# A four-layer convolution and attention stack on one Trainium2 core: the first image tensor also passed in channels first, and the biases of the linear attention as one 512-column product a bank

## The chip, the cores and the metric

One core of a Trainium2 chip runs the whole program. The metric is the device time of one execution in microseconds (us). The kernel before takes 10623.62 us, the median of three runs (10621.04 to 10631.18).

## What is computed

Four images of 64 x 64 positions with 128 channels, in f32, pass through four layers; each adds its result to its input. The change touches the first two alone.

- Layer 0 is a deformable attention. The image is normalized by groups of channels, multiplied into queries, keys and values, filtered by a 3 x 3 filter per channel, and from the filtered queries come offsets and masks for 4 groups of 9 taps. Each position then gathers its 36 sampled points (4 corners each), scores them against its query, and sums the values.
- Layer 1 is a linear attention over the whole image, with a normalization of its own and one of its result.

```python
qkv = x @ w_qkv + b_qkv                      # layer 0, x normalized before
...
attn = softmax(einsum('bgnc,bgckn->bgnk', q * SCALE, sampled_keys))
out = einsum('bgnk,bgckn->bgnc', attn, sampled_values) @ w_proj + b_proj
...
qkv = einsum('bhwc,cf->bhwf', x, w_qkv)      # layer 1, x normalized before
q = softmax(q, -1) * 32 ** -0.5; k = softmax(k, 1); v = v / n
context = einsum('bnhd,bnhe->bhde', k, v)
out = einsum('bhde,bnhd->bnhe', context, q) @ w_out + b_out
```

Layer 1 has no bias of its own on q, k and v; the one in the kernel comes from the normalization, whose mean is taken off behind the product instead of ahead of it.

## The kernel before, in words

`first_layers` (line 118) does layers 0 and 1. Its main loop runs over 128 tiles of 128 positions, 32 tiles an image. In each tile:

- POOL (line 467, `tile`) issues 36 indirect DMAs, which gather the sampled records into `rec[t % 2]`. With two such buffers, the gather of tile t may start once DVE has summed tile t-2, that is, at the end of line 935.
- DVE works on the gathered tile: keys by query (line 920), their sum (921), the scores (up to 925); then it waits for ACT's exp (line 706, `prob`), and goes on with line 928 to the sum of the values (line 935, `att_t`).
- PE turns and projects the result (lines 603 to 606), DVE adds the input (line 942), ACT stores it (line 712).

After each tile every engine takes one step of a side program, by `next(side)`. `sides` (line 313) gives its order: in the 32 tiles of image b there are first the 19 gaps of `points(b + 1)` (all that layer 0 needs before the gathers of the next image), and then the 11 gaps of `linear(b - 1)` (layer 1 of the image before). So `points(1)`, `points(2)` and `points(3)` have their gap 0 behind tiles 0, 32 and 64, and their gap 1 behind tiles 1, 33 and 65. `points(0)` runs ahead of the tiles as a prologue, and `linear(3)` behind them as an epilogue. `linear(0)` starts behind tile 51; its gap 7, with the "o" banks, lies behind tile 58.

Side work on PE and ACT is a list of jobs, each with its gap (`opening` and `beside` for layer 0, `lj` for layer 1). A job is one PSUM bank of 512 columns: PE fills bank `ps[n % 4]`, ACT copies it out, and PE may write that bank again once ACT has copied job n-4. In its own program ACT takes all copies of a gap before the exp of the next tile.

Jobs that the text speaks of:

- "x" (layer 0, gap 0): 4 PE transposes a bank (line 503) from the tokens `a_tok`, 8 banks, copied by ACT (line 631) to the image by channels `a_chan`. Out of it DVE takes the statistics in gap 1 (`spread`, line 726; bn_stats is line 729).
- "qkv" (layer 0, gap 1): 24 banks of one product each (line 514), copied by ACT (line 636). They wait for `spread`.
- "qv" (layer 1, gaps 1 to 4; 3, 5, 5 and 3 banks): two products of 256 columns (line 567), each followed by a product that adds the bias `brow` by a row of ones (line 568), copied by ACT (line 684).
- "o" (layer 1, gap 7; 8 banks): four products of 128 columns (line 594), each followed by one that adds the bias `bl_s` (line 595), copied by ACT (line 689).

Of the kernel before, what the change touches and what calls it, by code (L numbers as in the profile page):

```python
# [12 lines left out]
ACT = mybir.ActivationFunctionType  # L13
AX = mybir.AxisListType.X

P = 128
BATCH, H, W, C = 4, 64, 64, 128
N = H * W
# [99 lines left out]
def first_layers(nc, A, x, records, meta, mid, out):  # L118
# [9 lines left out]
    with ExitStack() as ctx:  # L128
# [10 lines left out]
        a_tok = tiles_at(R1)  # L139
# [55 lines left out]
        brow = st.sb("brow", [1, 2, C])  # L195
# [91 lines left out]
        opening = [("x", g, 0) for g in range(NG)]  # L287
        opening += [("qkv", (f, g), 1) for f in range(3) for g in range(NG)]
# [46 lines left out]
        def _(sp):  # L335
# [7 lines left out]
            def points(b):  # L343
# [4 lines left out]
                for r in (slice(0, P // 2), slice(P // 2, P)):  # L348
                    sp.dma_start(a_tok[r, :, :], batch(x, b)[r, :, :]).then_inc(a_x, 16)
# [132 lines left out]
        def _(pe):  # L482
# [3 lines left out]
            def points(b):  # L486
                done_act, done_offs, pj = b * PA, b * NG, plan(b)
                for gap in range(PG):
                    for n, (kind, at, own) in enumerate(pj):
# [10 lines left out]
                        if kind == "x":  # L500
                            pe.wait_ge(a_x, b * 80 + 80)
                            for t in range(4):
                                last = pe.transpose(bank[:, t * P:t * P + P], a_tok[:, 4 * at + t, :], id_s[:, :])
                        if kind == "qkv":
                            f, g = at
                            if n == NG:
# [33 lines left out]
            def linear(b):  # L540
                pe.wait_ge(l_x, b * 96 + 96)
                pe.wait_ge(l_act, b * LJ)
                for gap in range(LG):
                    for n, (kind, g, own) in enumerate(lj):
# [18 lines left out]
                        if kind == "qv":  # L563
                            for t in range(2):
                                o = bank[:, t * 256:t * 256 + 256].rearrange("p (f d) -> p f d", f=2)
                                i = 2 * g + t
                                pe.matmul(o, l_chan[:, i * P:i * P + P], lw_s[:, 0:3:2, :], start=True, stop=False)
                                last = pe.matmul(o, ones[:, :], brow[:, :, :], start=False, stop=True)
# [16 lines left out]
                        if kind == "o":  # L585
                            if g == 0:
                                pe.wait_ge(l_blk, b + 1)
                                pe.matmul(ps_c[:, P:2 * P], blocks[:, :], wo_s, start=True, stop=True).then_inc(l_mix, 1)
                                pe.wait_ge(l_mixc, b + 1)
                                pe.wait_ge(l_act, b * LJ + FIRST["o"])  # L590
                            for t in range(4):
                                i = 4 * g + t
                                o = bank[:, t * P:t * P + P]
                                pe.matmul(o, l_chan[:, i * P:i * P + P], mix, start=True, stop=False)
                                last = pe.matmul(o, ones[:, :], bl_s, start=False, stop=True)
# [15 lines left out]
        def _(act):  # L611

            def points(b):
                pj = plan(b)
                for gap in range(PG):
# [9 lines left out]
                    for n, (kind, at, own) in enumerate(pj):  # L625
# [4 lines left out]
                        if kind == "x":  # L630
                            ins = act.activation(a_chan[:, at * 512:at * 512 + 512], bank[:, :], ACT.Copy)
                        if kind == "qkv":
                            f, g = at
                            if n == NG:
                                act.wait_ge(a_norm, 2 * b + 2)
# [83 lines left out]
        def _(dve):  # L719
# [5 lines left out]
            def spread(sums, values, chain, act_sem, act_base, stat, gsum, var, std, nm, norm, pair, mean, cell, source):  # L725

                for g in range(NG):
                    dve.wait_ge(act_sem, act_base + g + 1)
# [37 lines left out]
            def points(b):  # L766
# [3 lines left out]
                spread(stats, a_chan, step_a, a_act, b * PA, a_stat, a_gsum, a_var, a_std, a_nm, a_norm, m2, mv, sc, b)  # L770
# [83 lines left out]
            def linear(b):  # L854
                yield
                spread(stats, l_chan, step_l, l_act, b * LJ, l_stat, l_gsum, l_var, l_std, l_nm, l_norm, m2, mv, sc, b)
# [3 lines left out]
                dve.tensor_copy(brow[:, :, :], ps_s[0:1, 128:512].rearrange("p (f d) -> p f d", f=3)[:, 0:3:2, :]).then_inc(l_norm, 1)  # L860
# [31 lines left out]
                dve.sem_inc(l_blk, 1)  # L892
                dve.wait_ge(l_mix, b + 1)
# [1450 lines left out]
def l0_arrays(i):  # L2344
    a = {n: np.asarray(i["L0_conv_" + n]) for n in ("w_qkv", "b_qkv", "w_dw", "b_dw", "pconv_off_w", "w_off", "b_off", "pconv_mask_w", "w_mask", "b_mask", "w_proj", "b_proj")}
    return dict(
# [93 lines left out]
```

## Time and profile before

| | |
|---|---|
| runs | 10623.62 us median of 3 (10621.04 to 10631.18) |
| the profiled execution | 10620.11 us, its span 10618.3 us |
| prologue (`points(0)`) | 0 to 317 us |
| the 128 tiles with their side work | 317 to 7618 us |
| epilogue (`linear(3)`) | 7618 to 7860 us |
| layers 2 and 3 | 7860 to 10618 us |
| busy over the span | PE 3786.1, DVE 5654.4, ACT 1430.5, POOL 4571.0 us |

The span runs from the first to the last instruction on the chip; the execution's own time is 1.8 us longer. Times in rows are counted from the start of the span. The timeline gives for an instruction its start, its duration, engine, line and operation, then how long the engine had been idle before it and what ended that. A releaser named "remote" or "issue" is one that the profile does not tie to an instruction of another engine.

### The profile page before, as it was taken

To read this page: it belongs to the slowest core of one execution; us is meant where nothing else is said; L and a number is where in the kernel's file an instruction comes from. 1 tells how busy PE (TensorE), PEld (TensorE's weight loads), DVE (VectorE), ACT (ScalarE), POOL (GpSimd) and SP (SyncE) were. 2 spreads that over 40 slices of the span, in tenths; PEclk is the share of its full clock that TensorE was granted. 3 is DMA by queue.
4 is the path that set the end of the run, shared out by engine and by line. 5 is a ranking of instruction groups with operands and counts; after the bars stand their busy time and mean duration, and the time that the engine had idled before them with its cause. 6 is when DMAs were issued, how large, how long until landed. Compare 5 with 4: busy or idle time off the path is not lost. (4 is left out here: it accounts for less than half of the span.)

```text
span 10618.3 us, 108724 instructions
## 1 busy us (share of the span) xinstructions
PE 3786.1 (36%) x42948; PEld 2618.7 (25%) x42948; DVE 5654.4 (53%) x6585; ACT 1430.5 (13%) x2619; POOL 4571.0 (43%) x4748
## 2 busy tenths in 40 slices
PE   5113100012202211130132132000267568699997
PEld 3001100000201110020111011000134346588885
DVE  5275754556664554657455445544444356455554
ACT  1000000000000000000000000000012133344442
POOL 0565667755565555656564564777400000000000
PEclk6555555555555555555555555555566778899998
DMA  4433363323336233424632332333220533222224
GB/s 78 115 100 84 96 161 104 108 81 101 83 107 149 82 88 92 110 74 108 151 92 78 97 90 79 106 100 100 66 41 0 195 68 78 78 67 67 65 67 168
DMA packets 973814, 1001.49 MB, mean 94 GB/s; under 512 B 417257, under 2 KB 794962, under 8 KB 969298
## 3 DMA queue, kind: packets, MB, share of 16 engines
q0 software_dynamic: 221184, 604.27, 19.6%
q1 hardware_dynamic: 703106, 350.65, 13.9%
q10 hardware_dynamic: 49104, 40.35, 1.3%
q8 instruction: 339, 5.55, 0.2%
q14 instruction: 81, 0.66, 0.0%
HBM read 797.88 MB, written 190.61 MB: 93 GB/s over the span
## 5 line engine op out<-in xcount | busy, mean ns | idle before, releaser
L467 POOL DMA_INDIRECT l_rec<-records,l_row x4608 | 4514.9, 980 | 3071.4 <-issue 1530.4
L603 PE MATMUL l_pso<-l_id,l_att_t 128*128 128x128 f32 x128 | 60.3, 471 | 5129.3 <-DVE l_att_t L935 2818.4
L603 PEld LDWEIGHTS l_pso<-l_id,l_att_t 128*128 128x128 f32 x128 | 23.7, 185 | 5176.5 <-DVE l_att_t L935 2850.6
L920 DVE TENSOR_TENSOR l_rec<-l_rec,l_psv 128x4608 f32<-128x4608 f32 x128 | 634.0, 4953 | 1024.3 <-DMA l_rec<-records,l_row 944.8
L935 DVE TENSOR_REDUCE l_att_t<-l_rec 128x128 f32<-128x4608 f32 x128 | 1004.4, 7847 | 4.4
L2191 DVE COPY l3p_mix<-l3p_ps 128x512 f32<-128x512 f32 x1024 | 660.0, 686 | 577.8 <-PE l3p_ps L2067 577.8
L928 DVE TENSOR_REDUCE l_total<-l_prob 128x4 f32<-128x36 f32 x128 | 24.4, 191 | 1626.9 <-ACT l_prob L706 1483.9
L2153 ACT ACTIVATE l3p_mix<-l3p_ps 128x512 f32<-128x512 f32 x1024 | 556.6, 596 | 664.1 <-PE l3p_ps L2067 664.1
L933 DVE TENSOR_TENSOR l_rec<-l_rec,l_psv 128x4608 f32<-128x4608 f32 x128 | 634.0, 4953 | 4.4
L921 DVE TENSOR_REDUCE l_dots<-l_rec 128x144 f32<-128x4608 f32 x128 | 634.0, 4953 | 4.4
L2067 PE MATMUL l3p_ps<-l3p_psi,l3p_ms 32*128 32x128 f32 x16384 | 611.7, 283 | 22.2 <-DVE l3p_mix L2191 17.4
L2067 PEld LDWEIGHTS l3p_ps<-l3p_psi,l3p_ms 32*128 32x128 f32 x16384 | 518.7, 186 | 181.7 <-ACT l3p_mix L2153 109.0
L2028 POOL COPY l3p_four<-l3p_fil 128x128 f32 (+1 forms) x64 | 18.7, 292 | 1199.5 <-PE l3p_psm L2120 1198.0
L764 DVE SCALAR_TENSOR_TENSOR l_psc<-l_area,l_wd,l_psc 128x512 f32<-128x512 f32 x504 | 381.0, 756 | 17.9
L706 ACT ACTIVATE l_prob<-l_score 128x36 f32<-128x36 f32 x128 | 29.5, 230 | 2544.7 <-DVE l_score L925 774.2
L2017 POOL MEMSET l3p_xs<- 128x4096 f32 x1 | 3.5, 3511 | 849.2 <-POOLq L55 849.2
L1386 POOL MEMSET l2b_res<- 128x512 f32 x1 | 0.5, 524 | 720.3 <-POOLq L55 720.3
L708 ACT ACTIVATE l_att_c<-l_pso 128x128 f32<-128x128 f32 x128 | 35.5, 277 | 2039.3 <-PE l_pso L603 1164.7
L942 DVE TENSOR_TENSOR l_done<-l_pso,l_res 128x128 f32<-128x128 f32 x128 | 37.4, 292 | 500.8 <-PE l_pso L606 393.0
L2084 PE MATMUL l3p_psy<-l3p_mix,l_mats 128*32 128x128 f32 x8192 | 259.7, 273 | 1.1 <-ACT l3p_yr L2162 0.8
L2084 PE MATMUL l3p_psy<-l3p_mix,l3p_xs 128*32 128x128 f32 x8192 | 259.0, 273 | 0.2 <-issue 0.2
L2084 PEld LDWEIGHTS l3p_psy<-l3p_mix,l_mats 128*32 128x32 f32 x8192 | 217.3, 108 | 21.1 <-issue 1.3
(360 smaller groups left out, 7230.7 us busy)
## 6 DMA issues: line engine op xcount, KB each, us to landing
l_rec<-records,l_row POOLq DMA_INDIRECT x4608
records<-l_area SPq DMA_DIRECT2D x96, 512.0 KB
l2b_w<-l_w SPq DMA_DIRECT2D x32, 1024.0 KB, 10.8
l_row<-meta SPq DMA_DIRECT2D x128, 154.0 KB
l_area<-x SPq DMA_DIRECT2D x16, 1024.0 KB
records<-l_rec SPq DMA_DIRECT2D x32, 512.0 KB
l_x_hat<-l3a_xout ACTq DMA_DIRECT2D x32, 512.0 KB, 4.2
l3p_xin<-l_x_hat SPq DMA_DIRECT2D x128, 128.0 KB, 3.1
```

The source lines that it names most:

```text
L467: pool.indirect_dma_start(out=rec[s % 2][:, k, :], out_offset=None, in_=records[b].rearrange("o g y x c d -> (o g y x) (c d)"), in_offset= ...
L603: pe.transpose(ps_a, att_t[:, :], id_s[:, :]).then_inc(s_att, 1)
L764: step_a(dve.scalar_tensor_tensor(acc if t < TAPS - 1 else to, window(f, g, t), wd_s[:, f, t:t + 1], acc, ALU.mult, ALU.add))
L920: step(dve.tensor_tensor(keys, keys, asked.broadcast_to([P, GROUPS, TAPS * CORNERS, HC]), ALU.mult))
L921: step(dve.tensor_reduce(flat, rec[two][:, :, :].rearrange("p k (c d) -> p (k c) d", c=CORNERS)[:, :, 0:HC], AX, ALU.add))
L933: step(dve.tensor_tensor(values, values, ps_w.rearrange("p (g m) -> p g m", g=GROUPS).unsqueeze(3).broadcast_to([P, GROUPS, TAPS * CORNERS ...
L935: step(dve.tensor_reduce(att_t[:, :].rearrange("p (g d) -> p g d", g=GROUPS), values.rearrange("p g m d -> p g d m"), AX, ALU.add))
L942: step(dve.tensor_tensor(done[two][:, :], ps_p, res[two][:, :], ALU.add))
L2067: mm = pe.matmul(bank.rearrange("p (x c e) -> p x c e", x=2, e=2)[:, i // 2, :, i % 2], ms[32 * g:32 * g + 32, 4 * q + i, :], psi[s][32 * ...
L2084: mm = pe.matmul(ps_y[32 * g:32 * g + 32, c, :], flat[:, 32 * m - 8 * r:32 * m - 8 * r + 32], mix[s][:, :, 2 * m + kind, :], start=r == 0 ...
L2153: act.activation(mix[t.side(0)][:, x:x + 2, :, :].rearrange("p x c e -> p (x c e)"), ps[(2 * q + h) % 3][:, 0, :], ACT.Copy).then_inc(s_se ...
L2191: dve.tensor_copy(mix[t.side(0)][:, x:x + 2, :, :].rearrange("p x c e -> p (x c e)"), ps[(2 * q + h) % 3][:, 1, :]).then_inc(s_setd, 1)
```

## The change

First part: a new input `x_chan` is the same image tensor, with channels first, laid out on the host. SP loads it straight to `a_chan` (two transfers of 64 rows with 16 KB a row, in place of two from `x` in pieces of 512 bytes). The 8 "x" jobs of each image, 32 transposes and 8 copies, are gone. DVE's `spread` waits for the load instead of ACT's copies, and the first "qkv" job carries the waits that job 8 had.

Second part: in the linear attention a bank gets its bias by one product of 512 columns ahead of the others. For "qv" that is 1 + 2 products in place of 4, for "o" 1 + 4 in place of 8. The bias row is therefore held twice (`brow`, two copies) and four times (`orow`, a new copy on DVE in gap 7, before its wait for `l_mix`); both rows now lie in parts of `area` that are free then. The columns that PE writes in a bank, 1024 with the bias, stay as they were.

```diff
@@ -192,7 +191,8 @@
         wo_s, ls_s, bl_s = wq_s[:, 0:C], wq_s[:, C:2 * C], wq_s[0:1, 2 * C:3 * C]
-        brow = st.sb("brow", [1, 2, C])
+        brow = area[0:1, 5 * N:5 * N + 4 * C].rearrange("p (t f d) -> p t f d", t=2, f=2)
+        orow = area[0:1, 2 * N:2 * N + 4 * C].rearrange("p (t d) -> p t d", t=4)
         bcol = st.sb("bcol", [P, 1])
@@ -284,8 +284,7 @@
         PG, LG = 19, 11
-        opening = [("x", g, 0) for g in range(NG)]
-        opening += [("qkv", (f, g), 1) for f in range(3) for g in range(NG)]
+        opening = [("qkv", (f, g), 1) for f in range(3) for g in range(NG)]
         opening += [("qt", g, 6) for g in range(NG)]
@@ -346,7 +345,7 @@
                 for r in (slice(0, P // 2), slice(P // 2, P)):
-                    sp.dma_start(a_tok[r, :, :], batch(x, b)[r, :, :]).then_inc(a_x, 16)
+                    sp.dma_start(a_chan[r, :], x_chan[b, r, :]).then_inc(a_x, 16)
                 sp.dma_start(wq_s[:, :], A["l0_w_qkv"]).then_inc(a_x, 16)
@@ -497,13 +496,10 @@
                             pe.wait_ge(a_act, done_act)
-                        if kind == "x":
-                            pe.wait_ge(a_x, b * 80 + 80)
-                            for t in range(4):
-                                last = pe.transpose(bank[:, t * P:t * P + P], a_tok[:, 4 * at + t, :], id_s[:, :])
                         if kind == "qkv":
                             f, g = at
-                            if n == NG:
+                            if n == 0:
+                                pe.wait_ge(a_x, b * 80 + 80)
                                 pe.wait_ge(a_stat, b + 1)
@@ -561,11 +557,11 @@
                         if kind == "qv":
+                            pe.matmul(bank[:, :], ones[:, :], brow[:, :, :, :].rearrange("p t f d -> p (t f d)"), start=True, stop=False)
                             for t in range(2):
...
                                 i = 2 * g + t
-                                pe.matmul(o, l_chan[:, i * P:i * P + P], lw_s[:, 0:3:2, :], start=True, stop=False)
-                                last = pe.matmul(o, ones[:, :], brow[:, :, :], start=False, stop=True)
+                                last = pe.matmul(o, l_chan[:, i * P:i * P + P], lw_s[:, 0:3:2, :], start=False, stop=t == 1)
                         if kind == "kt":
@@ -586,13 +582,12 @@
                                 pe.matmul(ps_c[:, P:2 * P], blocks[:, :], wo_s, start=True, stop=True).then_inc(l_mix, 1)
-                                pe.wait_ge(l_mixc, b + 1)
+                                pe.wait_ge(l_mixc, 2 * b + 2)
                                 pe.wait_ge(l_act, b * LJ + FIRST["o"])
+                            pe.matmul(bank[:, :], ones[:, :], orow.rearrange("p t d -> p (t d)"), start=True, stop=False)
                             for t in range(4):
                                 i = 4 * g + t
-                                o = bank[:, t * P:t * P + P]
-                                pe.matmul(o, l_chan[:, i * P:i * P + P], mix, start=True, stop=False)
-                                last = pe.matmul(o, ones[:, :], bl_s, start=False, stop=True)
+                                last = pe.matmul(bank[:, t * P:t * P + P], l_chan[:, i * P:i * P + P], mix, start=False, stop=t == 3)
                         last.then_inc(l_job, 1)
@@ -627,11 +622,9 @@
                         bank = ps[n % NB]
-                        if kind == "x":
-                            ins = act.activation(a_chan[:, at * 512:at * 512 + 512], bank[:, :], ACT.Copy)
                         if kind == "qkv":
                             f, g = at
-                            if n == NG:
+                            if n == 0:
                                 act.wait_ge(a_norm, 2 * b + 2)
@@ -722,10 +715,10 @@
 
-            def spread(sums, values, chain, act_sem, act_base, stat, gsum, var, std, nm, norm, pair, mean, cell, source):
+            def spread(sums, values, chain, ready, start, per, stat, gsum, var, std, nm, norm, pair, mean, cell, source):
 
                 for g in range(NG):
-                    dve.wait_ge(act_sem, act_base + g + 1)
+                    dve.wait_ge(ready, start + per * g)
                     ins = dve.bn_stats(sums[:, g, :], values[:, g * 512:g * 512 + 512])
@@ -767,7 +760,7 @@
                 yield
-                spread(stats, a_chan, step_a, a_act, b * PA, a_stat, a_gsum, a_var, a_std, a_nm, a_norm, m2, mv, sc, b)
+                spread(stats, a_chan, step_a, a_x, b * 80 + 80, 0, a_stat, a_gsum, a_var, a_std, a_nm, a_norm, m2, mv, sc, b)
                 dve.tensor_scalar(wn_s[:, :], wq_s[:, :], sc[:, 2:3], None, ALU.mult).then_inc(a_norm, 1)
@@ -853,11 +846,13 @@
                 yield
-                spread(stats, l_chan, step_l, l_act, b * LJ, l_stat, l_gsum, l_var, l_std, l_nm, l_norm, m2, mv, sc, b)
+                spread(stats, l_chan, step_l, l_act, b * LJ + 1, 1, l_stat, l_gsum, l_var, l_std, l_nm, l_norm, m2, mv, sc, b)
                 dve.tensor_scalar(lw_s[:, :, :], w_s[:, :, :], sc[:, 2:3], None, ALU.mult).then_inc(l_norm, 1)
...
                 dve.tensor_copy(bcol[:, :], ps_s[:, 2:3]).then_inc(l_norm, 1)
-                dve.tensor_copy(brow[:, :, :], ps_s[0:1, 128:512].rearrange("p (f d) -> p f d", f=3)[:, 0:3:2, :]).then_inc(l_norm, 1)
+                for t in range(2):
+                    ins = dve.tensor_copy(brow[:, t, :, :], ps_s[0:1, 128:512].rearrange("p (f d) -> p f d", f=3)[:, 0:3:2, :])
+                ins.then_inc(l_norm, 1)
                 yield
@@ -890,6 +885,7 @@
                 dve.sem_inc(l_blk, 1)
+                dve.tensor_copy(orow, bl_s.unsqueeze(1).broadcast_to([1, 4, C])).then_inc(l_mixc, 1)
                 dve.wait_ge(l_mix, b + 1)
@@ -2343,8 +2339,9 @@
     a = {n: np.asarray(i["L0_conv_" + n]) for n in ("w_qkv", "b_qkv", "w_dw", "b_dw", "pconv_off_w", "w_off", "b_off", "pconv_mask_w", "w_mask", "b_mask", "w_proj", "b_proj")}
+    x_chan = np.asarray(i["x"]).reshape(BATCH, N, C).transpose(0, 2, 1)
     return dict(
-        l0_w_qkv=a["w_qkv"], l0_b_qkv=a["b_qkv"].reshape(3, P).T, l0_w_dw=a["w_dw"].reshape(3 * C, TAPS), l0_b_dw=a["b_dw"].reshape(3, P).T,
+        x_chan=x_chan, l0_w_qkv=a["w_qkv"], l0_b_qkv=a["b_qkv"].reshape(3, P).T, l0_w_dw=a["w_dw"].reshape(3 * C, TAPS), l0_b_dw=a["b_dw"].reshape(3, P).T,
         l0_pconv_off=a["pconv_off_w"].transpose(4, 2, 3, 0, 1).reshape(3 * HC, 3, GROUPS * HC),
```

How the change moves instructions on ACT, from the end of tile 0 to the "qkv" copies of image 1 (before it `l_prob` is the exp of a tile, `l_att_c` and `l_psv` are copies of the tile loop, the DMA is the tile's store). Before:

```order
L706 ACTIVATE l_prob<-l_score 128x36
L708 ACTIVATE l_att_c<-l_pso 128x128
L699 ACTIVATE l_psv<-l_row 128x128
L712 DMA x<-l_done 128x128
L631 ACTIVATE l_area<-l_ps 128x512 x8
L706 ACTIVATE l_prob<-l_score 128x36
L708 ACTIVATE l_att_c<-l_pso 128x128
L699 ACTIVATE l_psv<-l_row 128x128
L712 DMA x<-l_done 128x128
L618 ACT_TABLE_LOAD
L618 ACTIVATE l_sc<-l_sc 128x1
L636 ACTIVATE l_area<-l_ps,l_bn 128x8x64 x24
```

With the change:

```order
L699 ACTIVATE l_prob<-l_score 128x36
L701 ACTIVATE l_att_c<-l_pso 128x128
L692 ACTIVATE l_psv<-l_row 128x128
L705 DMA x<-l_done 128x128
L699 ACTIVATE l_prob<-l_score 128x36
L701 ACTIVATE l_att_c<-l_pso 128x128
L692 ACTIVATE l_psv<-l_row 128x128
L705 DMA x<-l_done 128x128
L613 ACT_TABLE_LOAD
L613 ACTIVATE l_sc<-l_sc 128x1
L629 ACTIVATE l_area<-l_ps,l_bn 128x8x64 x24
```

The eight copies between the store of tile 0 and the exp of tile 1 are gone; the 24 "qkv" copies stand where they stood, between tile 1 and tile 2.

On PE, the start of the "o" job (gap 7 of `linear`; the first row is the projection of the tile before, the second the product for `mix`). Before, with the last two rows repeated:

```order
L606 MATMUL l_pso<-l_bo,l_ones 128x128
L588 MATMUL l_psc<-l_wq,l_blocks 128x128
L594 MATMUL l_ps<-l_area 128x128
L595 MATMUL l_ps<-l_wq,l_ones 128x128
L594 MATMUL l_ps<-l_area 128x128
L595 MATMUL l_ps<-l_wq,l_ones 128x128
```

With the change, again with the last two repeated:

```order
L601 MATMUL l_pso<-l_bo,l_ones 128x128
L584 MATMUL l_psc<-l_wq,l_blocks 128x128
L587 MATMUL l_ps<-l_area,l_ones 128x512
L590 MATMUL l_ps<-l_area 128x128 x4
L587 MATMUL l_ps<-l_area,l_ones 128x512
```

Eight products a bank have become five, in the same place.

## Rows read from the trace of the kernel before

**Rows 1.** Stretches of the span: start:end, us, then busy us (instructions) of PE, PEld, DVE, ACT, POOL, granted clock, DMA share, GB/s.

```profile
317.00:7618.00 7301.00, 1253.29 (x3376) 734.52 (x3376) 4004.85 (x2957) 374.25 (x814) 4514.86 (x4608) 0.52 0.37 100
7618.00:7860.00 242.00, 147.54 (x440) 88.00 (x440) 61.56 (x151) 44.67 (x64) 0.00 (x0) 0.58 0.16 31
```

**Rows 2.** Timeline of DVE in a tile without side work.

```profile
6934.21 4.95 DVE L920 TENSOR_TENSOR l_rec<-l_rec,l_psv 128x4608 f32<-128x4608 f32 x1 [22.28 <-DMA l_rec<-records,l_row]
6945.65 0.19 DVE L928 TENSOR_REDUCE l_total<-l_prob 128x4 f32<-128x36 f32 x1 [0.37 <-ACT l_prob L706]
...
6985.05 4.95 DVE L920 TENSOR_TENSOR l_rec<-l_rec,l_psv 128x4608 f32<-128x4608 f32 x1 [22.75 <-DMA l_rec<-records,l_row]
```

**Rows 3.** The page's costliest groups: busy us, mean ns | idle before, releaser.

```profile
L928 DVE TENSOR_REDUCE l_total<-l_prob 128x4 f32<-128x36 f32 x128 | 24.4, 191 | 1626.9 <-ACT l_prob L706 1483.9
```

**Rows 4.** Timeline of ACT between the tiles 0 and 1.

```profile
392.84 0.60 ACT L631 ACTIVATE l_area<-l_ps 128x512 f32<-128x512 f32 x1 [2.48 <-issue]
...
463.80 0.60 ACT L631 ACTIVATE l_area<-l_ps 128x512 f32<-128x512 f32 x1 [6.41 <-remote]
464.29 0.22 ACT L706 ACTIVATE l_prob<-l_score 128x36 f32<-128x36 f32 x1
```

**Rows 5.** Timeline of DVE: start of tile 1.

```profile
409.24 4.95 DVE L920 TENSOR_TENSOR l_rec<-l_rec,l_psv 128x4608 f32<-128x4608 f32 x1 [17.10 <-DMA l_rec<-records,l_row]
```

**Rows 6.** Timeline of POOL: first issues of tiles 3, 4, 35 and 67.

```profile
478.74 0.94 POOL L467 DMA_INDIRECT l_rec<-records,l_row  x1 [26.48 <-DVE l_att_t L935]
...
558.51 0.94 POOL L467 DMA_INDIRECT l_rec<-records,l_row  x1 [35.08 <-DVE l_att_t L935]
...
2224.45 0.95 POOL L467 DMA_INDIRECT l_rec<-records,l_row  x1 [21.18 <-DVE l_att_t L935]
...
4133.64 0.94 POOL L467 DMA_INDIRECT l_rec<-records,l_row  x1 [34.45 <-DVE l_att_t L935]
```

**Rows 7.** Timeline of POOL: an issue within tile 34.

```profile
2200.78 1.10 POOL L467 DMA_INDIRECT l_rec<-records,l_row  x1 [0.30 <-issue]
```

**Rows 8.** Timeline of ACT, gap 1: "qkv" copies of images 1 and 2.

```profile
493.51 0.69 ACT L636 ACTIVATE l_area<-l_ps,l_bn 128x512 f32<-128x512 f32 x1 [4.61 <-PE l_ps L514]
495.22 0.69 ACT L636 ACTIVATE l_area<-l_ps,l_bn 128x512 f32<-128x512 f32 x1 [1.02 <-issue]
...
509.01 0.69 ACT L636 ACTIVATE l_area<-l_ps,l_bn 128x512 f32<-128x512 f32 x1 [4.91 <-remote]
...
543.37 0.23 ACT L706 ACTIVATE l_prob<-l_score 128x36 f32<-128x36 f32 x1
...
2259.37 1.27 ACT L636 ACTIVATE l_area<-l_ps,l_bn 128x512 f32<-128x512 f32 x2 [25.30 <-remote]
```

**Rows 9.** Timeline of ACT and POOL: "o" copies of image 0, and tile 61.

```profile
3733.78 0.60 ACT L689 ACTIVATE l_area<-l_ps 128x512 f32<-128x512 f32 x1 [13.49 <-remote]
3760.39 1.08 ACT L689 ACTIVATE l_area<-l_ps 128x512 f32<-128x512 f32 x2 [26.02 <-remote]
...
3779.27 0.60 ACT L689 ACTIVATE l_area<-l_ps 128x512 f32<-128x512 f32 x1 [5.19 <-PE l_ps L595]
...
3794.81 0.94 POOL L467 DMA_INDIRECT l_rec<-records,l_row  x1 [40.50 <-DVE l_att_t L935]
```

**Rows 10.** Timeline of ACT: a "qv" copy of gap 2 and one of the epilogue.

```profile
3452.45 0.60 ACT L684 ACTIVATE l_area<-l_ps 128x512 f32<-128x512 f32 x1 [18.32 <-remote]
...
7726.11 0.60 ACT L684 ACTIVATE l_area<-l_ps 128x512 f32<-128x512 f32 x1 [4.00 <-PE l_ps L568]
```

**Rows 11.** Timeline of PE in layer 2: bias of 512 columns, then products of 128.

```profile
7907.52 2.07 PE L1085 MATMUL l2a_ps<-l2a_brow,l2a_ones 1*128 1x512 f32 x2
7909.52 2.08 PE L1088 MATMUL l2a_ps<-l2a_wkv,l2a_chan 128*128 128x128 f32 x8
```

**Rows 12.** Timeline of PE and DVE in the prologue.

```profile
21.54 5.91 PE L503 MATMUL l_ps<-l_id,l_area 128*128 128x128 f32 x32 [21.54 <-DMA l_bo<-l_b_proj]
...
23.43 1.44 DVE L729 BATCH_NORM_STATS2 l_stats<-l_area 128x6 f32<-128x512 f32 x2 [23.43 <-ACT l_area L631]
```

More of the change, by code:

```diff
@@ L115, in token_norm, with first_layers @@
     step(ins)
-def first_layers(nc, A, x, records, meta, mid, out):
+def first_layers(nc, A, x, x_chan, records, meta, mid, out):
     AHEAD = 4
@@ L136, in tiles_at @@
             return area[:, start:start + N].rearrange("p (t c) -> p t c", c=C)
-        a_tok = tiles_at(R1)
         a_chan = area[:, R2:R2 + N]
@@ L2356, in layers01 @@
     meta = nc.dram_tensor("meta", (BATCH, NT, P, META), F32).ap()
-    first_layers(nc, A, x, records, meta, mid, out)
+    first_layers(nc, A, x, A["x_chan"], records, meta, mid, out)
 def l1_arrays(i):
```

## The prediction, made before the changed kernel ran

> **What bounds the kernel now.** I read the stretches first, since the change touches only layers 0 and 1. The 128 tiles take 7301 us, in which POOL is busy for 4515 and DVE for 4005; the epilogue takes 242 [rows 1]. A tile without side work shows the beat: DVE starts on the next one 50.84 us later and has then waited 22.75 us for gathered data [rows 2]. The gathers set the pace there; DVE's 28 us fit inside. The beat itself is POOL's issue: 36 issues at 0.95 + 0.30 us make 45.0 us [rows 6], and at 1.10 + 0.30 they make 50.4 us [rows 7].
>
> But 128 tiles at 45 to 50 us are 5760 to 6450 us, not 7301. The rest is in the groups by cost: DVE's line 928 waits 1483.9 us for ACT's exp [rows 3], where a tile without side work has 0.37 us of it [rows 2]. ACT is not busy then (374 us in 7301 [rows 1]). The timeline of ACT shows what it does: between the tiles it stands at its side copies, and the exp is queued behind them. In gap 0 the eight "x" copies last from 392.84 to 464.40, and the exp of tile 1 follows at once [rows 4], though DVE had started on that tile at 409.24 [rows 5]. POOL may gather tile 3 only once tile 1 is summed, so it pauses for 26.48 us [rows 6]. That chain (side copies, exp, sum, gather) is what the change can shorten: not the busy time, but the pauses of POOL.
>
> The copies are slow in a way that the busy time does not explain. During POOL's issues of a tile a bank of one "qkv" product comes every 5.60 us (4.91 idle + 0.69), but every 1.71 us at the start of the gap, where POOL has only just begun [rows 8]. Of banks with more instructions, an "o" bank of eight products comes after 13.49 to 26.02 us idle while POOL issues, and after 5.19 once it has stopped [rows 9]. So I read it as a price for each PE instruction while gathers are issued, which is lifted soon after POOL stops: POOL stopped at 3794.81 - 40.50 = 3754.31, and two "o" copies came at 3760.39, 6 us later [rows 9].
>
> **The change, part by part.**
>
> *Prologue.* PE starts its "x" transposes at 21.54, released by the constants, and DVE its statistics at 23.43 behind the first copy [rows 12]. Without them DVE starts at 21.54, and the copies' beat no longer stretches it: 1.9 us and about 1, so -3 (0 to -6, as all of PE's x work is 5.91 [rows 12]). It is first in a serial chain, so it counts in full.
>
> *Gap 0 of images 1 to 3.* 8 copies and 32 transposes go. What lies behind them is the exp of the next tile. A free tile takes 11.44 us from line 920 to line 928 [rows 2]; from the exp to the next gather it takes 478.74 - 464.29 = 14.45 [rows 4, 6]. Tile 1 is thus summed at 409.24 + 11.4 + 14.5 = 435.1 instead of 478.7. POOL ends tile 2 at 478.74 - 26.48 = 452.26 [rows 6] and goes straight on: 26.2 us less. Late next is gap 1: the exp of tile 2 stands behind 24 "qkv" copies. It came at 543.37 [rows 8], 19.9 us after POOL's last issue of tile 3 (558.51 - 35.08 = 523.43 [rows 6]). Those copies now start 44 us earlier, while the end of tile 3's gather is 26 us earlier, so at least as many are through when POOL stops, and the next pause stays 35 us. Two things may take back a little. The first copy came 14.8 us after the pause ended in image 1 (493.51 - 478.74) and 34.9 us after it in image 2 (2259.37 - 2224.45) [rows 6, 8]; with the longer lead, three banks more are left when POOL stops, about 3 us. And a tile may be gathered at the longer beat, 5.4 us. I take 26 - 3 = 23 for image 1; for image 2 the pause is 21.2, and the copies have 25 us more of room, 22; for image 3 the pause is 34.5 [rows 6], less 3 and 5.4, 26. Together -71. Bounds: all of the pauses and 9 us in image 2 (28.8 us from POOL's stop to the exp there against 19.9), -91; for the other end see the first rival.
>
> SP's loads stay two transfers of 1 MB in sum, at the same place of its program and in longer pieces; they were hidden behind tiles and stay so. The load lies a tile ahead of gap 0, and `spread` a tile behind it: two tiles for a load that now must be there one tile earlier. I cost it at nothing.
>
> *"o" banks, linear(0) to linear(2).* After POOL stopped, copies came at 3760.39 (two) and the last at 3779.27, the last 5.19 + 0.60 = 5.79 us behind the one before it; 3761.5 to 3779.3 holds three such steps [rows 9]; the exp, the sum and POOL followed, with a pause of 40.50. With five instructions a bank in place of eight, a bank takes 5/8 of the time under the gather. From 3733.78 to 3754 that lets at least one or two more through, and of four banks that PE may run ahead all are done at the stop. I take the last three as gone: 3 x 5.79 = -17 each. If only their own length shrinks (below), it is 3 x 1.79 = -5.
>
> *"qv" banks.* Three instructions for four. The fifth bank of gap 2 came after 18.32 us of idle time [rows 10]; a quarter of that is 4.6, in each of two gaps of five banks. Part goes into pauses that others set, so -3 an image (+3 to -13; `brow` costs DVE a copy more, and it is on the chain of gap 1; nearest rows: 0.19 us for a small operation, 0.7 for 512 columns [rows 3, 12]). The new `orow` copy lies while DVE waits for PE's `mix` anyway.
>
> Three images at -17 - 3: -60 (bounds -6 and -90).
>
> *Epilogue, linear(3).* Here nothing gathers, PE is the bound (147.5 of 242 us [rows 1]) and ACT waits for each bank: a "qv" bank comes every 4.00 + 0.60 = 4.60 us [rows 10], an "o" bank every 5.79 [rows 9]. Both write 1024 columns, bias included. What the new form takes is in layer 2, where a bias of 512 columns takes 2.00 us to the next instruction, and four products of 128 columns (two records each) 2.08 [rows 11], so 4.0 us a bank. The clock is 1.2 GHz in both. That is 16 x 0.6 = 9.6 and 8 x 1.79 = 14.3, less some at the higher clock and 0.4 for the copy: -22 (-15 to -25).
>
> A rule speaks against this part. The Trainium skill ("TensorE: Matmul & The Clock Gate", Back-to-back issue gap) gives the gap between products as columns by the clock, N / 1.2 ns cold, whatever their number. By that rule 1024 columns cost the same in two pieces or eight, and part two is worth nothing. The rows disagree: 5.79, 4.60 and 4.0 us for the same columns [rows 9, 10, 11].
>
> **Sum:** -3 - 71 - 60 - 22 = -156. The profiled execution takes 10620.1, so 10464; the median lies 3.5 above that execution, hence **10467 us**.
>
> **Rivals.**
> 1. *The wait comes back in the next gap.* Where POOL no longer pauses before tile 3, none of the "qkv" copies falls into the free time behind a pause, in which they came every 1.71 us. Five of them must then run after the stop, 5 x 1.71 = 9 us an image: -17 - 12 - 25 = -54. In "o" the banks only shrink, -16 in sum. With -3 and -22: -95, 10529. For it: 25.30 us of idle before the copies of image 2 [rows 8]. Against it: 44 us of head start for 26.
> 2. *Columns alone are the price.* Part two gives nothing, -74 remain: 10550. Against it the three bank times above.
> 3. *All clean*, every bound at its good end: -6 - 91 - 90 - 22 = -209, 10414.
> 4. *Slower: the longer beat.* The gather has two beats, 45.0 and 50.4 us a tile. By the mean busy time of an issue, 4514.86 / 4608 = 0.980 [rows 1], between 0.945 and 1.10, some 22% of the tiles have the longer one. If pauses are what keeps the beat short, fewer pauses make more long tiles. At 156 / 5.4 = 29 tiles more the gain is gone; with 48 more it is 259 - 156 = +103, 10727. For it: the quiet tiles at 6934 us have the long beat [rows 2]. Against it: even in the tiles at 6934 us POOL needs no pause to issue 36 times, and the mean of 0.980 us says that three tiles in four have the short beat now, most of them with no pause just ahead, since DVE holds POOL up in a few gaps an image only.
> 5. *No effect:* the pauses are filled by whatever comes next (the "qkv" gap swallows all of gap 0's gain, and the gap of the token norm that of "o"); only the epilogue and prologue count, -25: 10599, just outside 0.2%; with a little lost elsewhere, "same".
>
> **How the numbers follow.** The forecast has 0.45, rival 1 0.24, rival 2 0.12, rival 3 0.09, rival 5 0.05, rival 4 0.05. The range takes in the first four and their bounds: 10400 to 10560. Within 0.2% (21 us, about what a measurement can tell from no change) lies part of rival 5 and some mixture with rival 4: 0.04. Slower by more: 0.04. Faster: 0.92.
>
> **What the changed profile would show.** Right: no wait of line 928 in tiles 1, 33 and 65, and no POOL pause before tiles 3, 35 and 67; the pauses before tiles 4, 36 and 68 about as long as before; the last "o" copy of linear(0) 6 us or less after POOL's stop, and tile 61's pause some 23 us; in the epilogue 4.0 us a bank of "qv" and of "o", and a stretch of about 220 us. The wait of line 928 for exp would fall from 1484 us by some 44 x 3 + 17 x 3 and more. Wrong: pauses before tiles 4, 36, 68 longer by what the earlier ones lost (rival 1 or 5), epilogue banks still at 5.79 (rival 2), a mean POOL issue above 0.98 us (rival 4).

## The result and the profile after

The changed kernel takes 10537.33 us, the median of four runs (10513.33 to 10541.06), against 10622.33 us (four runs); the ratio is 0.9914, 95% interval 0.9901 to 0.9926. That is 85 us less; 156 us less were forecast. The time lies in the range, 8 us above that of rival 1.

The two traces can be set side by side stage by stage (the end of a stage is that of its last DVE instruction):

| stage | before | after | difference | forecast |
|---|---|---|---|---|
| prologue, to the keys of tile 0 | 364.0 | 359.7 | -4.3 | -3 |
| `points(1)` to `points(3)`, from the end of tile 0, 32, 64 to that of tile 2, 34, 66 | | | -14.7, -7.9, -12.0 | -71 |
| "qv" gaps of linear(0) to linear(2), tiles 54 to 57, 86 to 89, 99 to 102 | | | +8.9, +12.5, +6.4 | -9 |
| "o" gaps, tiles 59, 91, 104 (the pauses are before tiles 61, 93, 106) | | | -17.5, -15.6, -17.0 | -51 |
| all 128 tiles to the end of tile 127 | 7254.0 | 7204.5 | -49.5 | -131 |
| epilogue, to the end of layer 1 | 210.0 | 178.9 | -31.1 | -22 |
| layers 2 and 3, not touched | 2790.3 | 2796.1 | +5.8 | 0 |

The parts of the tiles add up to -57; +7 us come in steps of under 2 us in other tiles. The stretch of the tiles in the changed kernel, in the columns of [rows 1], and DVE's wait for exp (us in total, times, longest):

```profile
317.00:7564.20 7247.20, 1175.89 (x3040) 659.68 (x3040) 4007.81 (x2963) 358.26 (x788) 4526.39 (x4605) 0.52 0.37 101
```

```profile
DVE l_total L924 <- ACT l_prob L699: 1489.1, 65, 66.7
```

The wait of DVE for exp did not fall: 1489 us where it was 1483.9 [rows 3]. The prediction said that it would fall by over 180. What was taken from some tiles came back in others.

POOL's first issues of tiles 4, 36, 57, 61 and 68, in this order by time, answer to [rows 6, 9]:

```profile
539.45 0.94 POOL L466 DMA_INDIRECT l_rec<-records,l_row  x1 [46.30 <-DVE l_att_t L931]
...
2287.68 0.94 POOL L466 DMA_INDIRECT l_rec<-records,l_row  x1 [50.42 <-issue]
...
3504.89 0.94 POOL L466 DMA_INDIRECT l_rec<-records,l_row  x1 [26.95 <-DVE l_att_t L931]
...
3761.62 0.94 POOL L466 DMA_INDIRECT l_rec<-records,l_row  x1 [23.05 <-DVE l_att_t L931]
...
4166.40 0.94 POOL L466 DMA_INDIRECT l_rec<-records,l_row  x1 [50.07 <-DVE l_att_t L931]
```

There is no row for tiles 3, 35 and 67, since their pauses are gone (26.5, 21.2 and 34.5 us [rows 6]), as forecast. But the next pause of each image grew: before tile 4 from 35.1 to 46.3, before tiles 36 and 68 from 44.1 and 33.8 to about 50. Two pauses together went from 61.6 to 46.6 in image 1. In images 2 and 3, tiles 35 and 67 also got the longer beat (49.4 and 49.9 us for 44.7), which took 5 to 7 us back in each. Tile 57 has a pause of 26.95 where it had 7.6, and tile 61 one of 23.05 for 40.50 [rows 9]: the one is the loss at "qv", the other the gain at "o".

ACT's timeline in gap 1 of image 1 shows where the next pause grew ([rows 8] before):

```profile
464.12 1.84 ACT L629 ACTIVATE l_area<-l_ps,l_bn 128x512 f32<-128x512 f32 x3 [23.62 <-remote]
...
471.76 0.69 ACT L629 ACTIVATE l_area<-l_ps,l_bn 128x512 f32<-128x512 f32 x1 [4.91 <-PE l_ps L510]
...
508.86 0.69 ACT L629 ACTIVATE l_area<-l_ps,l_bn 128x512 f32<-128x512 f32 x1 [4.91 <-remote]
...
524.30 0.23 ACT L699 ACTIVATE l_prob<-l_score 128x36 f32<-128x36 f32 x1
```

Tile 1 was summed at 430.1, 5 us earlier than forecast (4 of them because tile 1 itself starts earlier, with the prologue), but the first copy came 34 us later (464.12), not 14.8. DVE's statistics themselves were as quick as before: from the first bn_stats to line 97 they took 8.4 us in both kernels. What came late is behind them: twelve memsets (8.9 us in place of 1.2) and the last small DVE instruction ahead of the copies, which waits for a short product of PE. In image 2 this way was as long before (35 us). The last instruction, before, then with the change:

```profile
492.87 0.16 DVE L779 TENSOR_TENSOR l_bn<-l_pss,l_bq 128x3 f32<-128x3 f32 x1 [1.33 <-DVE l_area L776]
```

```profile
461.96 0.16 DVE L772 TENSOR_TENSOR l_bn<-l_pss,l_bq 128x3 f32<-128x3 f32 x1 [9.62 <-remote]
```

That still leaves no fewer copies done when POOL stops: 8, 11 and 10 of the 24 in images 1 to 3, where it was 8, 4 and 8. The loss comes after the stop. POOL's last issue of tile 3 ends at 493.2; the copies go on at 5 us a bank until 508.86, and the exp comes 31 us behind the stop, where it was 19.9. In images 1 to 3, copies still came 4 us or more apart up to 16, 21 and 22 us after the stop, in the kernel before up to 2, 10 and 2 us. What differs ahead of the stop is for how long POOL had issued without a pause: four tiles, 16 and 6 with the change, one tile in each image before. In the middle of this late stretch no gather is issued and no byte is moved (columns of [rows 1]):

```profile
498.00:508.00 10.00, 4.15 (x4) 1.00 (x4) 0.00 (x0) 1.38 (x2) 0.00 (x0) 0.50 0.00 0
```

PE is busy for 4.15 of these 10 us, so its own work does not fill them either. Whatever holds up the short instructions outlasts the gathers themselves; what it is, no run shows.

The "qv" gaps show another way to lose a pause ([rows 10] before). Gap 2, then gap 3, of linear(0):

```profile
3409.57 0.60 ACT L677 ACTIVATE l_area<-l_ps 128x512 f32<-128x512 f32 x1 [3.41 <-issue]
...
3455.71 0.60 ACT L677 ACTIVATE l_area<-l_ps 128x512 f32<-128x512 f32 x1 [16.20 <-remote]
```

The banks of gap 2 now all come at 4.0 us, so tile 54 ends 18 us earlier, and POOL goes on to tile 56 without a pause (10.5 before). Then the second and third bank of gap 3 come 16.8 us apart and the fourth after 13.3; before, its first four came at 4.6. Tile 55 loses 27.

In the epilogue, a "qv" copy early and late, and the last "o" copy ([rows 9, 10] before):

```profile
7606.66 0.60 ACT L677 ACTIVATE l_area<-l_ps 128x512 f32<-128x512 f32 x1 [1.51 <-PE l_ps L564]
...
7656.16 0.60 ACT L677 ACTIVATE l_area<-l_ps 128x512 f32<-128x512 f32 x1 [3.41 <-PE l_ps L564]
...
7714.53 0.60 ACT L682 ACTIVATE l_area<-l_ps 128x512 f32<-128x512 f32 x1 [3.41 <-PE l_ps L590]
```

Both bank kinds take 4.01 us, as the price from layer 2 said [rows 11]; the first five "qv" banks ran at the higher of TensorE's two clocks, 2.1 us each, where the kernel before had two such (2.3 and 2.5 us).

### The profile page after: what moved, and what is told of

Its sections match the earlier page's. It is cut to its first block and busy times, and to the rows that moved or that the text cites. A ratio compares the mean times of both kernels' runs of the same rounds, so it can differ in the third digit from the quotient of the medians.

```text
span 10539.2 us, 107779 instructions
## 1 busy us (share of the span) xinstructions
PE 3679.2 (35%) x42500; PEld 2522.4 (24%) x42500; DVE 5657.8 (54%) x6593; ACT 1410.3 (13%) x2586; POOL 4585.7 (44%) x4748
```

## Experiments

Runs were taken in sets, each with the kernel before beside the new kernels. The next four kernels ran on the chip with number 11; the number for the first result is not known.

**Part one alone.** The changed kernel with the bias products, `brow` and `orow` as before:

```diff
-                            pe.matmul(bank[:, :], ones[:, :], brow..., start=True, stop=False)
+                                last = pe.matmul(o, ones[:, :], brow[:, :, :], start=False, stop=True)
```

> Part one alone (image by channels as an input; biases as before). Theory: each image gets what its tiles show in the changed kernel, -4 prologue, -15, -8, -13 = -40 us, and nothing else moves: about 10583 us, the pauses of the linear gaps as before (10.5 and 7.6 us before tiles 56 and 57). Rival (the two parts disturb each other, for instance through the gathers' beat): the images gain 60 or more without part two, 10560 or less.

10563.62 us, ratio 0.996 (0.9943 to 0.9977); its set ran wider than the first one, with the kernel before at 10608.14 (10584.91 to 10641.27). By the trace the tiles 1, 33 and 65 gain 43 to 51 us each and the tiles behind them lose 28 to 37: -16, -8, -14 net, -38. The pauses before tiles 4, 36 and 68 are 45.3, 49.9 and 48.9, the same as with both parts. So the small gain of part one is its own; nothing of it is lost to part two. The "qv" gaps did not stay as they were, though their code did: the pauses before tiles 56 and 57 are 5.4 and 17.6, together 5 more than before, and the three groups of "qv" gaps lose 4.5, 3.0 and 6.8 us.

**Part two alone.** The kernel before with the new "qv" and "o" banks:

```diff
-                                last = pe.matmul(o, ones[:, :], bl_s, start=False, stop=True)
+                            pe.matmul(bank[:, :], ones[:, :], orow..., start=True, stop=False)
```

> Part two alone (biases as one product a bank; transposes as before). Theory: 'o' gives -17 in each of linear(0) to linear(2), 'qv' costs +7 to +12 in each, the epilogue gives -25: together about -45, 10578 us. Rival (the loss in the 'qv' gaps belongs to where part one has moved the tiles): 'qv' costs nothing here, -75, 10548 us.

10534.94 us, ratio 0.9924 (0.9901 to 0.9947), about -80. The trace shows the mechanism as expected: each of the three "qv" pairs costs, tile 54 ends 18.1 us earlier and tile 55 27.1 later, and each "o" gap gains 17. At the end of tile 127 it stands at -37, the epilogue gives -28, the rest lies in layers 2 and 3, which were not touched. The measured time alone is nearer to the rival; the trace contradicts the rival, since the loss is there without part one.

The two parts alone do not add up to the change: their ratios multiply to 0.9884, and the change has 0.9914. The traces show where this can come from. In the tiles that belong to none of the three kinds of gap in the table, the changed kernel is 7 us behind the kernel before, and part one alone is 16 and part two alone 10 ahead of it. Differences of this size between two single traces are not the work of a part.

**Old "qv" banks inside the tiles.**

```diff
-                            pe.matmul(bank[:, :], ones[:, :], brow..., start=True, stop=False)
+                            if b == BATCH - 1:
+                                pe.matmul(bank[:, :], ones[:, :], brow..., start=True, stop=False)
...
+                                if b < BATCH - 1:
+                                    last = pe.matmul(o, ones[:, :], brow[:, t, :, :], start=False, stop=True)
```

> The changed kernel with the 'qv' banks of linear(0) to linear(2) as before (four products), new in the epilogue alone. Theory: the shorter 'qv' banks of gap 2 take away the POOL pause before tile 56, and the copies of gap 3 then lie in an unbroken gather and cost 27 us; with the old banks the pause is back and the tiles end 28 us earlier: about 10510 us, slack of tiles 54 and 55 at 47 and 50 us again. Rival (fewer instructions always help, the loss in these gaps comes from the second copy of the bias row or from chance in the gathers): 10537 or some us more.

10494.18 us, ratio 0.9891 (0.9869 to 0.9914). That looks like the theory, but the trace says otherwise. POOL before tile 56, and a copy of gap 3 behind it:

```profile
3434.17 0.94 POOL L466 DMA_INDIRECT l_rec<-records,l_row  x1 [3.86 <-issue]
```

```profile
3468.86 0.60 ACT L680 ACTIVATE l_area<-l_ps 128x512 f32<-128x512 f32 x1 [20.41 <-remote]
```

The pause did not come back: 3.9 and 23.5 us before tiles 56 and 57 make 27.4, with the new banks 0.3 and 27.0 make 27.3, in the kernel before 10.5 and 7.6 made 18.1. The three groups of gaps lose 8.8, 10.6 and 6.4 us, as with the new banks. So the loss is not bound to the new form. My theory of its cause fell; that of the spell behind a pause did not. Over the traces so far, the time of a tile 55, 87 or 100 from keys to sum runs against POOL's pause just as its copies begin: with 7.6 to 10.5 us of pause it is 45 to 52 us, with 3.9 to 5.4 it is 60 to 66, with 0.3 it is 69. The 34 us that this kernel is ahead of the changed one at the end of tile 127 come elsewhere, 30 of them in the tiles that neither part touches. 19 belong to tiles 60, 92 and 105, with the token norm: its 102 DVE instructions took 32.1, 39.2 and 30.7 us in the three images against 42.9, 46.4 and 48.1, for 20 us of work. Why, stays open. Its interval overlaps that of the changed kernel, so that it is better isn't shown either.

**"x" banks by one product.** In the kernel before, and the image isn't turned:

```diff
-                            for t in range(4):
-                                last = pe.transpose(bank[:, t * P:t * P + P], a_tok[:, 4 * at + t, :], id_s[:, :])
+                            last = pe.matmul(bank[:, :], id_s[:, :], a_tok[:, 4 * at:4 * at + 4, :]..., start=True, stop=True)
```

> The kernel before, each 'x' bank made by one product of 512 columns with the identity in place of four transposes of 128: same columns, fewer instructions, more passes; the image then is not turned, so the output is another. Theory (a price for each PE instruction under the gather): the copies of gap 0 come every 5 us and not every 10.5, the last at about 435 us in place of 463.8, and DVE's wait for exp in tile 1 falls from 44 to some 15 us. Rival (a price by column and pass, or by copy): 10 us or more a bank, as before.

```profile
417.59 0.60 ACT L630 ACTIVATE l_area<-l_ps 128x512 f32<-128x512 f32 x1 [5.00 <-issue]
423.89 0.60 ACT L630 ACTIVATE l_area<-l_ps 128x512 f32<-128x512 f32 x1 [5.70 <-issue]
```

10606.54 us, one run, against 10608.14. The first three copies are quick, then they come 4.9 to 6.3 us apart in place of some 10 (7 steps in 71 us). The last comes at 423.89 in place of 463.80 [rows 4], earlier than the 435 expected, and tile 1 has 29.6 us from keys to sum (25.3 is free). The same 512 columns and the same copy on ACT cost about half, with one product for four transposes. So columns are not the price; the number of PE instructions has a part in it. In records of the trace, of which an f32 product leaves two and a transpose one, it is 2.8 and 2.5 us each, and 2.8 in the new "qv" banks of six records at 16.8 us. The old "o" banks don't fit that: sixteen records, and one of them came 14.1 us behind the one before it [rows 9].

This alone gives image 1 -14.5 us, as much as taking all of "x" away: what lies beyond is handed to gap 1. It also settles what the "qv" loss does not come from. This kernel has the linear attention of the kernel before, with one copy of the bias row, and it loses 9.3, 13.3 and 6.8 us in the three groups of "qv" gaps, where the changed kernel loses 8.9, 12.5 and 6.4. Tile 54 ends 8.7 us earlier, the pause before tile 56 is 1.7 us, and tile 55 takes 67.7 us. So the loss needs neither the new "qv" form nor the second copy of the row. Of the six traces of kernels that took over 10400 us, that of the kernel before is the only one without it, and there is one such trace of it: whether the kernel or that one execution is the exception, isn't shown.

**Tile 3 by plain transfers, statistics in gap 0, split copies.** Three kernels on the changed one, and a fourth, the split on the kernel with the old "qv" banks:

```diff
+                        pool.dma_start(rec[s % 2][:, k, :], flat[P * k:P * k + P, :]).then_inc(s_rec[s % 2], 16)
```

> The changed kernel, with the 36 gathers of tile 3 alone replaced by 36 plain transfers of the same size from POOL (128 rows of 1 KB that lie together; tile 3 then computes on other records, so its output is another). It lies beside the 24 'qkv' copies of image 1, which now last from 464 to 523 us. Theory (the issue of indirect gathers is what slows the instructions of the other engines): the copies come at PE's own pace, under 2 us each, from about 450 to 480, and the exp of tile 2, now at 524, comes 35 to 45 us earlier. Rival (the bytes moved are what slows them): the copies stay at 4.9 to 5.6 us a bank while the transfers last, some 25 us, and the exp comes less than 15 us earlier.

```diff
-        opening = [("qkv", (f, g), 1) for f in range(3) for g in range(NG)]
+        opening = [("qkv", (f, g), (NG * f + g) // 12) for f in range(3) for g in range(NG)]
```

> The changed kernel with the statistics in the now empty gap 0 and the 'qkv' banks as 12 in gap 0 and 12 in gap 1. Theory (copies are cheap in the 20 us behind a POOL pause and dear in an unbroken gather): the first twelve make a pause before tile 3, the other twelve use the free spell behind it, and an image's tile 2 is done about 20 us earlier: -60, near 10477 us. Rival (the number of copies sets it, wherever they lie): the same sum of waits, 10537 within 15 us.

```diff
                 act.activation(prob[:, :], score[:, :], ACT.Exp).then_inc(s_exp, 1)
+                if t:
+                    next(side)
```

> The changed kernel; ACT makes the first half of each gap's side copies ahead of the next tile's exp, as now, and the second half between that exp and its copy of the tile's result. Nothing else moves and nothing is left out. Theory (the tiles lose time because the exp queues behind all the copies, while ACT stands idle for the 14.5 us between exp and result): each of some 12 overfull gaps an image gains up to 14 us where POOL pauses for it, 250 us in sum with a wide margin, 10290 us. Rival (the wait only moves from exp to the result's copy): within 30 us of 10537.

> The same split on the kernel with the old 'qv' banks inside the tiles. Theory: the split decides more than the form of the 'qv' banks, whose copies are now half behind the exp, so both split kernels lie within 20 us of each other. Rival: the 43 us between the unsplit ones stay.

The split also moves the Sigmoid of gap 12 and the Sqrt of gap 8 ahead of their gaps' copies.

These four ran on chip 7, and there the kernel before took 9179.3 us (9166.57 to 9186.79), 14% less than on chip 11. The new kernels took, in the order above, 9118.4 (one run), 9123.96 (ratio 0.9947, 0.993 to 0.9963), 9116.7 (0.9932, 0.9916 to 0.9949) and 9127.4 (0.994, 0.9923 to 0.9956). None of the expectations could be tested: the slow copies they were aimed at were not there. That the two split kernels lie within 20 us of each other, as the theory said, says nothing here for the same reason.

**Both kernels again.** No edit, on chip 8.

> The kernel before, for its trace. The kernel before took 10608 us in the first set of runs and 9179 in the second, in which the 'qkv' copies came every 0.86 us under the gathers. Theory (the slow arrival of side copies belongs to the chip of the first set, not to the kernel): where the whole takes about 9180 us, the eight 'x' copies of gap 0 end within 15 us, DVE waits for exp in hardly any tile and POOL has no pauses but those of DVE's own work; where it takes about 10610, all is as in the first trace. Rival: the faster time comes from the gathers themselves (a beat below 45.0 us a tile).

> The changed kernel. Theory: where the kernel before takes about 9180 us, POOL does not pause for the copies in either kernel, so the tiles gain next to nothing and the prologue (-4) and the epilogue (-31) are the whole gain: -35 to -55 us. Where it takes about 10610, -86 as before. Rival (the change is worth the same share on either): -80 us.

The kernel before took 9176.66 us (seven runs), the changed one 9122.88, ratio 0.9948 (0.9929 to 0.9967): 54 us less, within the -35 to -55 of the theory, and the rival's -80 lies outside the interval. The last "x" and "qkv" copies of gaps 0 and 1 in the kernel before:

```profile
395.37 2.29 ACT L631 ACTIVATE l_area<-l_ps 128x512 f32<-128x512 f32 x4 [0.25 <-PE l_ps L503]
...
469.38 0.69 ACT L636 ACTIVATE l_area<-l_ps,l_bn 128x512 f32<-128x512 f32 x1 [0.17 <-PE l_ps L514]
```

And POOL's group and DVE's wait, of the kernel before, then of the changed one:

```profile
L467 POOL DMA_INDIRECT l_rec<-records,l_row x4608 | 4404.6, 956 | 1746.8 <-issue 1400.3 <-DMA l_row<-meta 315.0 <-DVE l_att_t L935 21.4
...
DVE l_total L928 <- ACT l_prob L706: 147.4, 128, 21.8
```

```profile
L466 POOL DMA_INDIRECT l_rec<-records,l_row x4608 | 4401.2, 955 | 1719.2 <-issue 1394.1 <-DMA l_row<-meta 308.9 <-DVE l_done L938 11.3
...
DVE l_total L924 <- ACT l_prob L699: 103.0, 128, 8.2
```

The same instructions, under the same gathers at 1.25 us an issue, now come as fast as PE makes them: 0.86 us a "qkv" bank for 5.6. DVE waits 147 us for exp in place of 1484, and POOL 21 us for DVE where it was 1225. The rival (faster gathers) accounts for a smaller part: POOL's work took 4404.6 us for 4514.9, and its time between issues 1400 for 1530, together 240 of the 1450 us. 10 tiles took over 48 us to issue, where it was 35. Here the change gives -6 in the prologue, -25 in all tiles (POOL's pauses behind the "o" gap, 4.2 to 4.4 and 2.5 us an image, are gone: 20 of the 25) and -27 in the epilogue. Beyond the prologue part one gives next to nothing: at the ends of tiles 2 and 34 the changed kernel is 6.1 and 6.7 us ahead.

**Split copies and tile 3, a second time.** No new edit, on chip 12.

> The changed kernel with the copies split around the exp, a second time, for a chip on which the kernel before takes about 10610 us: the first time it ran where the copies are quick anyway. Theory and numbers as for split_copies: there each overfull gap gains up to 14 us, 250 us in sum with a wide margin, near 10290; where the kernel before takes about 9180, the gathers are the bound throughout and it comes out as the first time, about 9117.

> Tile 3 fetched by plain transfers, a second time, for the same reason. Where the kernel before takes about 10610 us: if the issue of indirect gathers slows the other engines, the exp of tile 2 comes 35 to 45 us before the 524 us of the changed kernel; if the bytes do, less than 15 us earlier. Where it takes about 9180: as the first time, exp of tile 2 at about 467 us.

The kernel before took 9176.08 us, the split 9131.1 (ratio 0.9952, 0.9935 to 0.9968), tile 3 by plain transfers 9131.16. DVE's wait for exp in the split kernel:

```profile
DVE l_total L936 <- ACT l_prob L709: 47.3, 128, 0.7
```

0.7 us at most, where the changed kernel has up to 8.2: the split does take the exp out of the queue. But where POOL no longer waits, that buys nothing over the changed kernel. What it is worth at 10610 us wasn't tried.

## Why the prediction was right, and where it wasn't

- *What bounds it.* Right: the gathers set the beat, the exp behind the side copies makes the pauses, and the change acts by them. Right also, where the copies are slow, that fewer PE instructions for the same columns make a bank cheaper under the gathers, and that there is a quick spell behind a pause: "x as one product" shows the first, the pauses ahead of tiles 56, 88 and 101 the second.
- *"x" term.* The size was wrong by half, -35 for -71. The sentence was "Those copies now start 44 us earlier ... so at least as many are through when POOL stops, and the next pause stays 35 us." They start 29 us earlier in image 1, because the way to the first copy took 19 us more and not 3. Even so as many were through at the stop (8, 11 and 10 for 8, 4 and 8). The step that failed is the last one: the prediction took from [rows 9] that the price is lifted soon after POOL stops, 6 us. Behind one tile of gathers that nearly held (slow copies up to 2, 10 and 2 us after the stop). Behind four tiles or more without a pause the copies stayed slow for 16 to 22 us after the stop, the exp came 31 us behind it, not 19.9, and the pauses before tiles 4, 36 and 68 grew by 11, 6 and 16 us. Rival 1 put 9 us on an image, for another reason (that more copies are left at the stop); the size came near, the reason did not.
- *"qv" term.* Wrong in sign, +28 for -9. I priced the banks one gap at a time and wrote "Part goes into pauses that others set"; that a lost pause before tile 56 makes the next gap's banks dear was not in the sum. The loss is in the trace; that the change causes it is not shown, since a kernel with the old linear attention has it too.
- *"o" term.* Right, -50 for -51. Tile 61's pause was said to be some 23 us and is 23.05. Here the next gaps have few copies, so nothing was handed on.
- *Epilogue.* Right in kind, -31 for -22: 4.0 us a bank as priced, most of the rest from more banks at the higher clock. Rival 2 falls: 5.79 and 4.60 us went to 4.0 with the columns the same. By the formula that the prediction took from the Trainium skill ("TensorE: Matmul & The Clock Gate", Back-to-back issue gap) they would have stayed. But the prediction read that section too narrowly: it gives the formula for an isolated product and says itself that it under-counts at small N. The bank times agree with that in part. With the bias in pieces too, a bank took 5.79 us in eight of 128 columns and 4.60 in four of 256; behind one bias product of 512 columns, four pieces of 128 and two of 256 both take 4.01. Small pieces alone cost nothing here, but small pieces in turn with the bias do.
- *Beat.* Rival 4 took place in small: mean issue 0.983 us (4526.39 / 4605) for 0.980, 12 us in tiles 34, 35 and 67. Its argument had more to it than the prediction granted. In both traces most of the long tiles stand in two runs, 24 to 34 and 112 to 127, and each run begins with the fifth or sixth tile behind POOL's last pause. Tile 67, whose pause is gone, is now the sixth behind one, and took 49.9 us for 44.7.
- *Sign and cases.* The sign was right. That the time lies 8 us from rival 1 is luck: rival 1 had -54 for "x", -16 for "o", -3 for "qv" and -22 for the epilogue, and the trace has -35, -50, +28 and -31. The range held because it took in the rivals' bounds.

Open: what makes instructions of PE, ACT and DVE come slowly under and behind the gathers in some sets of runs and not in others. The experiment on it (tile 3 by plain transfers) ran only where they come quickly. That neither an issue nor a transfer need be under way is shown by the stretch from 498 to 508 us.

## What to carry to other kernels

Where side work queues ahead of a step of the main loop, don't cost a cut gap by gap: follow what the pause that goes away was good for in the next gap. Here half of the gain was left. The work outside the loop paid at least what it was priced at (-31 for -22 us), and there one product of 512 columns for the bias is worth having. A gain by taking waits away should be measured on more than one chip: here 85 us of 10620 became 54 of 9177, and 35 and 33 of them are prologue and epilogue. And one trace of a kernel does not tell its gaps' lasting cost: gaps that no edit touched moved by 10 us and more.

## What was not expected of the hardware

The same program took 10608 us on chip 11, and 9179, 9177 and 9176 us on chips 7, 8 and 12. Each chip ran one set, so that the chip itself is the cause is likely and not shown. Nearly all of the difference lies in the tiles (7254 us against 5820 from the keys of tile 0 to the end of tile 127, by the traces of the first result and of chip 8; layers 2 and 3 took 2790 and 2776). In the slower runs short instructions of three engines came late while POOL issued gathers, and up to 22 us after it had stopped: PE and ACT as above, and the 102 DVE instructions of the token norm took 43.4 us (21 busy) for 19.2. Their lateness comes in steps of about 0.7 us (idle times of 4.21, 4.91 and 5.61).
